# One fp32 operand for the router: half the products, and two more copies out of PSUM

## The reference, cut to what matters

```python
inh = jax.nn.sigmoid(x @ Wr / temperature)          # Wr is 256 x 8
in_zone = (inh >= GOLDEN_LOWER) & (inh <= GOLDEN_UPPER)
dist = jnp.abs(inh - GOLDEN_CENTER)
w = jnp.exp(-dist / 0.1) * in_zone                  # if no expert is in the zone:
_, top2 = jax.lax.top_k(jnp.exp(-dist / 0.3), 2)    # weights of the nearest two
...
gate = jnp.einsum('btd,edi->beti', x, Wg)
up = jnp.einsum('btd,edi->beti', x, Wu)
h = jax.nn.silu(gate) * up
e_out = jnp.einsum('beti,eid->betd', h, Wd)
out = jnp.einsum('bte,betd->btd', weights, e_out)
```

## Time and profile before

| | before |
|---|---|
| median of 3 runs | 1487.56 us (1487.32 to 1488.09) |
| profiled execution | 1487.54 us |
| its span | 1485.8 us, mean granted clock 0.997 |
| TensorE matmul busy | 98% of the span |
| VectorE, ScalarE, GpSimd busy | 68%, 43%, 29% |

### The profile page before, as it was taken

How to read it: one execution, slowest core, us unless ns; L and a number is a source line. 1 busy time by engine, 2 the same in 40 slices (tenths; PEclk the granted TensorE clock), 3 DMA queues, 4 the chain that set the end, 5 groups by cost and what they waited for, 6 DMA issues and landing times. The chain is left out here.

```text
span 1485.8 us, 37233 instructions
## 1 busy us (share of the span) xinstructions
PE 1462.7 (98%) x14438; PEld 1276.4 (86%) x14438; DVE 1003.5 (68%) x2397; ACT 632.5 (43%) x1157; POOL 427.4 (29%) x621
## 2 busy tenths in 40 slices
PE   7899999999999999999999999999999999999997
PEld 7788888888888888888888888888888888888886
DVE  6748567576676767667586675766667676675765
ACT  5434534444344443534435343443434445344332
POOL 1402414123241322414133141232413124141230
PEclk9999999999999999999999999999999999999999
DMA  5100000000000000000000000000000000000000
GB/s 172 58 2 15 14 0 14 14 14 14 0 28 0 14 14 14 14 0 14 14 14 14 0 14 14 14 14 0 28 0 14 14 14 14 0 15 16 2 8 22
DMA packets 25345, 24.59 MB, mean 17 GB/s; under 512 B 2016, under 2 KB 25056, under 8 KB 25312
## 3 DMA queue, kind: packets, MB, share of 16 engines
q1 hardware_dynamic: 25312, 24.13, 5.1%
HBM read 15.74 MB, written 8.39 MB: 16 GB/s over the span
## 5 line engine op out<-in xcount | busy, mean ns | idle before, releaser
L1013 DVE TENSOR_TENSOR late<-late,up_ps 128x512 f32<-128x512 f32 x256 | 174.9, 683 | 153.7 <-PE up_ps L440 149.3
L790 ACT ACTIVATE late<-gate_ps 128x512 f32<-128x512 f32 x256 | 152.6, 596 | 278.8 <-PE gate_ps L440 277.7
L440 PE MATMUL down_ps<-w_hi,h_hi 128*128 128x256 f32 x976 | 264.6, 293 | 0.0
L709 ACT ACTIVATE h_hi<-late 128x512 fp32r<-128x512 f32 x256 | 161.4, 630 | 222.0 <-DVE late L1013 221.9
L440 PE MATMUL down_ps<-w_hi,h_lo 128*128 128x256 f32 x976 | 253.9, 282 | 0.0
L1247 POOL TENSOR_TENSOR rms_in<-rms_in,minus_half 128x16 f32<-128x16 f32 x32 | 93.4, 2918 | 493.7 <-DVE rms_in L961 493.7
L902 DVE TENSOR_TENSOR h_lo<-late,h_hi 128x512 fp32r<-128x512 f32 x256 | 175.7, 686 | 65.4 <-ACT h_hi L709 65.4
L1035 DVE SCALAR_TENSOR_TENSOR late<-down_ps,route,late 128x256 f32<-128x256 f32 x364 | 158.6, 477 | 90.3 <-PE down_ps L440 87.8
L440 PE MATMUL gate_ps<-ft_hi,w_hi 128*128 128x512 f32 x512 | 204.0, 398 | 1.4 <-ACT ft_hi L709 0.8
L440 PE MATMUL gate_ps<-ft_hi,w_lo 128*128 128x512 f32 x512 | 203.0, 396 | 0.0
L440 PE MATMUL up_ps<-ft_hi,w_hi 128*128 128x512 f32 x512 | 199.7, 390 | 0.0
(11 more groups left out here) (172 smaller groups left out, 2420.6 us busy)
## 6 DMA issues: line engine op xcount, KB each, us to landing
xs<-in_x SPq DMA_DIRECT2D x32, 256.0 KB, 2.9
out_rows<-late SPq DMA_DIRECT2D x32, 256.0 KB, 2.2
late<-in_wg SPq DMA_DIRECT2D x7, 256.0 KB, 3.3
late<-in_wu SPq DMA_DIRECT2D x7, 256.0 KB, 4.3
late<-in_wd SPq DMA_DIRECT2D x6, 256.0 KB, 4.4
late<-in_wkv_t SPq DMA_DIRECT2D x1, 512.0 KB, 4.1
x<-in_wd SPq DMA_DIRECT2D x2, 256.0 KB, 5.2
late<-in_wq_t SPq DMA_DIRECT2D x1, 256.0 KB, 4.6
```

The lines of the kernel that those rows point to most:

```text
L440: last = nc.tensor.matmul(dst, lhs, rhs, start=n == 0, stop=n == len(terms + low_terms) - 1)
L709: return nc.scalar.activation(dst, src, ACT.Copy)
L790: nc.scalar.activation(h_f[:, m, :], gate_ps[:, :], ACT.Silu).then_inc(silu_ready[0], 1)
L1013: nc.vector.tensor_tensor(h_f[:, m, :], h_f[:, m, :], up_ps[m][:, :], ALU.mult).then_inc(h_ready[0], 1)
```

## The change

The router no longer reads the two parts. A new buffer name, `ft_whole`, is a view of `rows` in the shape of the transposed tokens. A new step, ("ft_whole",), stands at place 27 and at the end of block 0's order for ScalarE. It waits for VectorE's `ft_ready` of each half and copies the half from PSUM, unrounded, into `ft_whole`; the second copy signals the new counter `ft_whole_ready`. The router waits for that counter in place of `ft_ready` and makes its products of `ft_whole` alone. All other engines do nothing at the new step.

```diff
@@ STEPS
     [("ft", 0), ("ft", 1), ("ft_out", 0), ("ft_out", 1)],
-    [],
+    [("ft_whole",)],
@@ FIRST_ACT
-             ("unit", 20), ("unit", 21), ("wo", 1), ("unit", 22), ("unit", 23), ("ft_out", 0), ("ft_out", 1)]
+             ("unit", 20), ("unit", 21), ("wo", 1), ("unit", 22), ("unit", 23), ("ft_out", 0), ("ft_out", 1), ("ft_whole",)]
@@ buffers and counters
+        ft_whole = rows[:, :, :].rearrange("p t n -> p (t n)").rearrange("p (k n) -> p k n", k=KT)
+        ft_whole_ready = counter("ft_whole_ready", 1)
@@ TensorE, att_step
                 elif kind == "r":
-                    reach(pe, ft_ready, a, 2)
-
-                    for n, (k, part) in enumerate((k, part) for k in range(KT) for part in (ft_hi, ft_lo)):
+                    reach(pe, ft_whole_ready, a, 1)
+
+                    for k in range(KT):
                         for t in range(TILES):
                             last = nc.tensor.matmul(dst[D * t:D * t + D, 0, 0:P], wr_pad[:, k, :],
-                                                    part[:, k, t * P:t * P + P].bitcast(f32), start=n == 0, stop=n == 2 * KT - 1)
+                                                    ft_whole[:, k, t * P:t * P + P], start=k == 0, stop=k == KT - 1)
@@ ScalarE, att_step
+                elif kind == "ft_whole":
+
+                    for p in range(2):
+                        reach(act, ft_ready, a, p + 1)
+                        last = copy(ft_whole[:, :, p * 2 * P:(p + 1) * 2 * P], att_half(("ft", p), a))
+                    last.then_inc(ft_whole_ready[0], 1)
```

## The result

| | before | after |
|---|---|---|
| median of 6 runs each | 1487.89 us (1487.32 to 1489.1) | 1481.36 us (1480.55 to 1482.31) |
| ratio after / before | | 0.9955, 95% interval 0.9943 to 0.9967 |
| profiled execution, its span | 1487.54, 1485.8 us | 1481.9, 1480.2 us |

The change takes 6.5 us off. The first two lines of the page after, against the earlier trace rows: ScalarE has 32 instructions and 17 us of work more, TensorE 256 matmuls and as many weight loads fewer.

The account below looks back on a forecast made before the run. TensorE's instruction stream was taken to bound the kernel. 15 blocks x 0.43 us = 6.45 us off, copies and block 0 counted as nothing, gave 1487.54 - 6.45 = 1481.1 us, range 1479.8 to 1483.8.

Parts of the forecast that it names:

- What bounds: From the second block to the end TensorE's instruction stream is the path; it was busy 98% of the span.
- The term of the sum: At the router, 16 of 32 matmul records a block go: two middle steps, 0.22 + 0.21 = 0.43 us per block.
- The copies: Two ScalarE copies into rows, 1.09 us, end 1.8 us before the router asks; costed at nothing.
- What is late next: Behind the router, down(7), x transposes and expert 1's gate products keep 1.3, 1.5 and over 0.8 us spare.
- Rival D: Gain given back at a later TensorE wait behind the router; wholly given back, 1487.5 us; chance 0.03.
- Block 0: First block gains nothing: its x transposes wait for ScalarE's normalisation, so 0.43 us becomes 0.3 to 0.4 us more waiting.
- B (doubled passes): At the router, unrounded fp32 operands need twice the passes, so two groups cost as four: 1487.5 us; chance 0.04.
- the bound at the scores step's price: Router groups of eight cost 0.256 us in place of 0.215: gain 0.38 us a block, 1481.8 us.
- C: TensorE waits at the router for copies delayed by ScalarE table loads: 1492.0 us; chance 0.03.
- The estimate by the 25 ns floor: At the router, 16 records a block at 25 ns each: 0.40 us a block, 6.0 in all, 1481.5 us.

Follow-up runs that it names:

- three to four pairs: The changed kernel with its pair of copies made three or four times, each pair behind the one before: 1486.94 us with three, 1505.39 us with four.
- the later comparison: The changed kernel, unedited, timed once more beside the kernel before: 1482.36 us, ratio 0.9961.
- the doubled products: The changed kernel with every router product of the unrounded operand made twice: 1488.05 us, ratio 1.0003 to the kernel before.
- after, shifted code: The changed kernel with four more warming matmuls in block 0: 1481.82 us, ratio 0.9957 to the kernel before.
- half the products again, shifted: The changed kernel with only the router's k = 0 products and four more warming matmuls in block 0: 1478.48 us, ratio 0.9933 to the kernel before.
- the half router alone: The kernel before without the low part's router products, nothing copied: 1481.92 us, ratio 0.9963.
- two pairs: The changed kernel with its pair of copies made twice, one pair behind the other: 1481.72 us, ratio 0.9952 to the kernel before.
- half the products again: The changed kernel with only the router's k = 0 products, 4 a block: 1481.48 us, ratio 0.9964 to the kernel before.

## Why the prediction was right, point by point

**What bounds.** TensorE's stream, and it alone. Leaving out the low part's products with no other edit gave 5.8 us; adding the copies with no other edit gave 0.3 us, which is within the interval.

**The term of the sum.** Predicted 0.22 + 0.21 = 0.43 us a block from the distances between starts; the periods give 0.423, the router's stretch 1.01 - 0.57 = 0.44. Reading the durations (0.40 us a group) would have given nearly twice that. The two middle steps were the right ones to take: entry and exit stayed.

**The copies.** Predicted 1.09 us for two, ending 1.8 us ahead of the router; measured 1.09 and 1.93. The prediction had each us of lateness at 15 us; the step from three to four pairs has 18.5 us for 1.11, so 16.6 an us: it had left out block 0, which pays as well once the copies are that late.

**What is late next.** Down(7,1) came at 781.04 with its add done at 779.51, 1.5 us spare where 1.3 was forecast; the x transposes at 782.48 with the rows ready at 780.95, 1.5 us as forecast; silu(0,1) ends at 781.61, 0.9 us ahead of those transposes. Rival D had no place.

**Block 0.** "Gives nothing" was right for the router's own 0.43 us, which became waiting: 0.3 to 0.4 us more were forecast, and from the logit transpose to the x transposes it is 1.14 us (65.28 to 66.42) in place of 0.36, so 0.78 more. The chain that it waits for was said not to depend on the router. That step failed, if by a small sum: VectorE's `h_lo` subtraction does depend on the router, and held up GpSimd's step. It cost 0.36 us once, which the sum didn't have.

**The total.** Forecast 1481.1 us, measured 1481.36, and 1482.36 in the later comparison; both lie in 1479.8 to 1483.8. A small part of the agreement is luck: by the spans of the profiled executions the gain is 5.6 us, 0.85 less than the 6.45 of the sum, of which 0.70 us is block 0 and the way to block 1. Of this only 0.36 us has a cause that the traces show.

**Bounds and rivals.** B (doubled passes) and the bound at the scores step's price were refuted by the doubled products. For C to be felt at all the copies had to come 1.93 us later than they do; with three pairs it just begins. The estimate by the 25 ns floor of the Trainium skill's page "TensorE: Matmul & The Clock Gate" (section "Wait — 56ns, not 53.3ns?"), 1481.5, can't be told from the forecast: it gives 6.0 us where the two comparisons gave 6.5 and 5.6. Going by the period, 0.423 us for 16 records is 26.4 ns a record, between that floor and the 27 ns of the rows. But this trace does not bear that page's floor out as one for every matmul, and the measurement decides: the 64x64 records of the scores step start 2.05 / 128 us = 16 ns apart, and those of the output step 0.90 / 64 us = 14 ns. That the router's pace lies close to 25 ns is therefore no sign that the page's floor sets it; why it is 27 ns stays open.

## What to carry to other kernels

Where one engine runs without a wait for a whole period, an edit to it is worth the distance between the starts of what goes, times the number of periods, and work moved to another engine is free up to a deadline that can be read off the timeline: here 1.9 us, and one to one behind it. Read the gain from the period, because the total also holds things that the edit doesn't mean to touch: a collision in the first block, or where the code of a first pass comes to lie. If a comparison by the total denies an edit what its period shows, look for waits on "issue" in code that runs for the first time, see whether a packet of the instruction queue ended just ahead of them, and shift the code by a few harmless instructions before giving the edit up.

## What the runs showed of the hardware

The stalls of 1.3 us without a releaser were not expected. They fell into the densest stretch of instructions in the kernel (64 records in about 1 us, each with its weight load) and only in code on its first pass. The DMA view of the profile after shows when TensorE's program may be on its way: one packet of the instruction queue q8 between 170 and 1340 us, while the loop repeats, of 22 in the whole execution.

```profile
q8 instruction: 22, 0.36, 0.1%
```

```profile
q8 instruction: 1, 0.02, 0.0%
```

The Trainium skill's page "Runtime: NRT & Kernel Launch" (section "Instruction fetch mechanics") describes a buffer for each engine that is refilled in blocks of 16 KiB by its own DMA queue, and calls the cost of a boundary mostly hidden. The packets here are of that size (0.36 MB / 22). No packet lies in the stalls themselves, but one ends just ahead of each. The table has the packet of q8 that comes around the 64 records at about 109 us, from the DMA records of each trace: its start and end, the start of the 64 records, the time until the next group starts, and where the records go on after the break.

| kernel | packet | 64 records start | until the next group | go on at |
|---|---|---|---|---|
| before | 105.64 to 106.86 | 108.91 | 0.90 | no break |
| after, shifted code | 106.22 to 107.18 | 109.55 | 0.90 | no break |
| after | 107.88 to 108.81 | 109.52 | 1.02 | 110.46 |
| half the products again, shifted | 106.87 to 107.88 | 108.52 | 1.02 | 109.46 |
| the half router alone | 107.34 to 108.59 | 109.02 | 1.28 | 110.22 |
| two pairs | 107.99 to 108.92 | 109.32 | 1.30 | 110.54 |
| half the products again | 109.33 to 110.41 | 109.60 | 2.23 | 111.70 |

The later the packet ends in relation to the records, the longer the break; the other six profiles fit in. Wherever there is a break, TensorE goes on 1.3 to 1.7 us after the packet's end. At the second stall the packet runs from 1360.27 to 1361.57 us and the records go on at 1363.01, 1.4 us behind it; with the shifted code it ended at 1356.94, 1.4 us ahead of its 64 records (1358.36), and there was no break. The edit and the shift move the packet's start against the code behind it: from 3.3 us ahead of the 64 records (before) to 1.6 (after) and 0.3 (half the products again), and with the shift back to 1.6 there and to 3.3 in after. So a refill that comes late is what all these profiles agree on, at both stalls. It is still read across profiles: no run held back a packet with the code left as it is. Nor do the views say whose program q8 carries; it has 23 packets in the four kernels with 16 router products a block and 22 in the nine with fewer, so its number goes with TensorE's instructions.
